# One exponential per wavelength over a ring of two slots, and three wavelengths summed in one column group

## What is computed

```python
cos_pm = jnp.cos(phase_modulators)
def wl_step(acc, wl):
    cpm, iw = wl
    m = cpm[None, :, None, None]
    scores = jnp.einsum('bhqd,bhkd->bhqk', Q * m, K * m) * SCALE
    scores = scores * jnp.cos(KERR * scores * scores)      # KERR = 2.7e-12
    attn = jax.nn.softmax(scores, axis=-1)
    out = jnp.einsum('bhqk,bhkd->bhqd', attn, V)
    return (acc + out * iw, None)
acc, _ = jax.lax.scan(wl_step, acc0, (cos_pm, interference_weights))
...
x = _layernorm(x + attention(x)); x = _layernorm(x + experts(x))
```

## Time and profile before

| | |
|---|---|
| time, median of 3 runs | 7213.8 us (7212.1 to 7214.84) |
| time of the profiled execution | 7212.97 us |
| its span, first to last instruction | 7211.4 us |
| ScalarE busy | 6960.2 us, 97% |
| VectorE busy | 5712.5 us, 79% |
| TensorE busy | 5963.4 us, 83% |
| mean granted TensorE clock | 0.942 of 2.4 GHz |

### The profile page before, as it was taken

How to read it: one execution, slowest core, us unless ns; L and a number is a source line. 1 busy time by engine, 2 the same in 40 slices (tenths; PEclk the granted TensorE clock), 3 DMA queues, 4 the chain that set the end, 5 groups by cost and what they waited for, 6 DMA issues and landing times.

```text
span 7211.4 us, 126028 instructions
## 1 busy us (share of the span) xinstructions
PE 5963.4 (83%) x46020; PEld 2136.2 (30%) x46020; DVE 5712.5 (79%) x7952; ACT 6960.2 (97%) x2227; POOL 116.5 (2%) x243
## 2 busy tenths in 40 slices
PE   6788787877888888888888888888888888888877
PEld 2222222222232333332332332332332332332335
DVE  4777778777788888888888888888888888888873
ACT  3999999999999999999999999999999999999992
POOL 0000000000000000000000000000000000000000
PEclk7999999999999999999999999999999999999998
DMA  2000000000010010010100010000110000000101
GB/s 59 4 4 3 4 4 4 2 4 7 24 29 20 24 29 22 21 29 20 30 29 19 24 29 17 27 29 16 30 31 18 27 28 15 29 26 19 29 18 36
DMA packets 61110, 151.22 MB, mean 21 GB/s; under 512 B 10272, under 2 KB 28576, under 8 KB 60320
## 3 DMA queue, kind: packets, MB, share of 16 engines
q1 hardware_dynamic: 59808, 142.14, 6.9%
q0 software_dynamic: 768, 1.57, 0.1%
HBM read 132.66 MB, written 11.01 MB: 20 GB/s over the span
## 4 chain that ended last, share of the span: by engine, by line
ACT 54%; issue 25%; PE 10%; ACTq 6%; DVE 4%; DMA 0%; SPq 0%; DVEq 0%
ACT ring L558 54%; PE pv L627 5%; ACTq L553 5%; DVE scores L768 1%; ACTq L554 1%; PE sc L1094 1%; PE tr L1102 1%; PE pv L634 1%; PE sc L610 1%; ACT L572 0%; ACTq L546 0%; PE sc L591 0%; DMA scores<-in_L_attn_x 0%; DVE vprobs L793 0%; DVE vprobs L792 0%
## 5 line engine op out<-in xcount | busy, mean ns | idle before, releaser
L558 ACT ACTIVATE ring<-scores 128x4096 f32<-128x4096 f32 (+3 forms) x2048 | 6752.4, 3405 | 40.3 <-DVE scores L768 32.8
L627 PE MATMUL pv<-ring,vh 128*32 128x512 f32 x30720 | 4023.3, 638 | 1131.4 <-ACT ring L558 1120.3
L627 PEld LDWEIGHTS pv<-ring,vh 128*32 128x32 f32 x30720 | 1009.9, 115 | 3810.8 <-issue 2119.1
L800 DVE COPY numer<-pv 128x512 f32<-128x512 f32 x512 | 352.6, 689 | 487.3 <-PE pv L634 482.9
L768 DVE COPY scores<-sc 128x1024 f32<-128x1024 f32 (+1 forms) x512 | 602.2, 1218 | 82.3 <-PE sc L610 79.4
L758 DVE TENSOR_REDUCE rowmax<-sc 128x1 f32<-128x1024 f32 x512 | 601.9, 1218 | 50.5 <-PE sc L591 49.1
L794 DVE SCALAR_TENSOR_TENSOR vprobs<-ring,vprobs 128x1024 f32<-128x1024 f32 x512 | 627.3, 1225 | 17.6
L793 DVE SCALAR_TENSOR_TENSOR vprobs<-vprobs,vbits 128x1024 f32<-128x1024 f32 x512 | 627.3, 1225 | 17.4
L792 DVE SCALAR_TENSOR_TENSOR vprobs<-ring 128x1024 f32<-128x1024 f32 x512 | 623.3, 1217 | 2.9
L634 PE MATMUL pv<-vpower,vlast 128*32 128x512 f32 x2048 | 532.3, 595 | 0.0
L634 PE MATMUL pv<-vprobs,vlast 128*32 128x512 f32 x2048 | 529.6, 592 | 0.0
(11 more groups left out here) (158 smaller groups left out, 2669.8 us busy)
## 6 DMA issues: line engine op xcount, KB each, us to landing
tile_w<-in_L_ffn_w SPq DMA_DIRECT2D x192, 512.0 KB, 3.9
qt<-q_scratch SPq DMA_DIRECT2D x256, 36.0 KB
kt_<-k_scratch SPq DMA_DIRECT2D x256, 36.0 KB
ring<-in_L_ffn_w SPq DMA_DIRECT2D x2, 2048.0 KB, 11.8
scores<-in_L_attn_x SPq DMA_DIRECT2D x4, 512.0 KB, 5.2
q_scratch<-qt SPq DMA_DIRECT2D x4, 512.0 KB, 3.8
k_scratch<-kt_ SPq DMA_DIRECT2D x4, 512.0 KB, 4.2
v_scratch<-vv SPq DMA_DIRECT2D x4, 512.0 KB, 3.7
```

The lines of the kernel that those rows point to most:

```text
L558: nc.scalar.activation(ring[:, i % SLOTS, 0:cols], scores[:, bass.ds(n % 2, 1), half * CK:(half + 1) * CK, :].rearrange("p o k s -> p (o k ...
L627: last = nc.tensor.matmul(sums, vh[:, buf, half * CK + k, :], ring[:, 2 * half + w2, col:col + HALF], start=(half == 0 and k == 0), stop=( ...
```

## The change

ScalarE makes all of a wavelength in one activation of 7680 numbers: key tiles 0 to 6, and of tile 7 the first 512 queries. The ring becomes two slots of a whole wavelength. The first activation of a head waits for all eight key tiles of scores, not for four.

VectorE makes the other 512 queries of tile 7 for every wavelength, still two wavelengths at a time: the first operation, whose factor differs, is split in two of 512; the others work on 2 x 512 numbers. Its schedule moves by one step (bit operations in odd steps, polynomials in even ones), and gets a wait for TensorE's step 2 x pair - 3.

TensorE weighs one wavelength a step. The four column groups are now (query half, half of the key tiles); each step has 15 matmuls from the ring and two for VectorE's part, both in the last group. The values stand in `vh` at columns 18 to 26 of 50, zeros around them; a window of 32 columns shifted by 9 puts three wavelengths one below the other in the same 32 partitions, so `pv` is filled and copied once for three wavelengths ("fill"; six a head: 3, 3, 3, 3, 2, 2). Turning a fill also adds the two halves of the key tiles, in a matmul with `fold` in place of the identity (4 matmuls a fill, 64 columns each). `normalise` runs three times a head, on two fills. The products of the tile work get a bank of their own (`tr[:, 1]`) and lose some waits.

```diff
-NCH = 2 * W
 CK = KT // 2
-SLOTS = 4
+SLOTS = 2
+OWN = HALF
+CHUNK = KT * S - OWN
+VR = D + 1
+STACK = 3
+VW = VC + (STACK - 1) * VR
+VAT = (STACK - 1) * VR
+FILLS = ((0, 1, 2), (3, 4, 5), (6, 7, 8), (9, 10, 11), (12, 13), (14, 15))
+NF = len(FILLS)
+FILL_OF = [f for f, ws in enumerate(FILLS) for _ in ws]
+GROUPED = [(f, f + 1) for f in range(0, NF, 2)]
...
-        ring = sb("ring", [P, SLOTS, CK * S])
-        vh = sb("vh", [P, 2, KT, VC])
+        ring = sb("ring", [P, SLOTS, KT * S])
+        vh = sb("vh", [P, 2, KT, VW])
...
-        vbits = sb("vbits", [P, S], I32)
-        vmant = ring[:, SLOTS - 1, (CK - 1) * S:CK * S]
-        vlast = sb("vlast", [P, 2, 2, VC])
+        vbits = sb("vbits", [P, 2, OWN], I32)
+        vmant = ring[:, :, CHUNK:KT * S]
...
-                    for i in range(8):
-                        pair, half, w2 = i // 4, (i // 2) % 2, i % 2
-                        w, chunk = 4 * quad + 2 * pair + w2, NCH * n + 8 * quad + i
-                        if i in (0, 2):
-                            act.wait_ge(sc_free, USES * n + ROW_USE + 1 + CK * (half + 1))
-                        if half == 0:
-                            act.reg_load(scale[w2], scale_bits[:, bass.ds(w * H + n % H, 1)])
+                    for i in range(4):
+                        w, chunk = 4 * quad + i, W * n + 4 * quad + i
+                        if i == 0:
+                            act.wait_ge(sc_free, USES * (n + 1))
+                        act.reg_load(scale[i % 2], scale_bits[:, bass.ds(w * H + n % H, 1)])
                         act.wait_ge(slot_free, chunk + 1)
                         apart(act)
-
-                        cols = CK * S - (S if half == 1 and w2 == 1 else 0)
-                        nc.scalar.activation(ring[:, i % SLOTS, 0:cols],
-                                             scores[:, bass.ds(n % 2, 1), half * CK:(half + 1) * CK, :].rearrange("p o k s -> p (o k s)")[:, 0:cols],
-                                             ACT.Exp, scale=scale[w2]).then_inc(probs_ready, 1)
+                        nc.scalar.activation(ring[:, i % SLOTS, 0:CHUNK],
+                                             scores[:, bass.ds(n % 2, 1), :, :].rearrange("p o k s -> p (o k s)")[:, 0:CHUNK],
+                                             ACT.Exp, scale=scale[i % 2]).then_inc(probs_ready, 1)
...
+        def weigh_values(pe, n, buf, w):
+
+
+            f = FILL_OF[w]
+            j, pair, w2 = FILLS[f].index(w), w // 2, w % 2
+            first, final = j == 0, w == FILLS[f][-1]
+            window = slice(VAT - j * VR, VAT - j * VR + VC)
+            if w == 0:
                 pe.wait_ge(vh_ready, n + 1)
+            pe.wait_ge(probs_ready, W * n + w + 1 + START)
             for k in range(CK):
                 for g in range(G):
+                    qh, kh = g // 2, g % 2
+                    kt = kh * CK + k
+                    if kt == KT - 1 and qh == 1:
                         continue
+                    last = nc.tensor.matmul(pv[g * VC:(g + 1) * VC, f % 2, :], vh[:, buf, kt, window],
+                                            ring[:, w % SLOTS, kt * S + qh * HALF:kt * S + (qh + 1) * HALF],
+                                            start=(first and k == 0), stop=(final and k == CK - 1))
+            for part, (stream, step) in enumerate(((vpower, POWER_STEP), (vprobs, VSTEPS))):
+                if w2 == 0:
                     pe.wait_ge(vexp_step, VSTEPS * (8 * n + pair) + step)
+                last = nc.tensor.matmul(pv[(G - 1) * VC:G * VC, f % 2, :], vlast[:, buf, part, window],
+                                        stream[:, pair % 2, w2 * OWN:(w2 + 1) * OWN], start=False, stop=(final and part == 1))
+            last.then_inc(slot_free, 1)
+
+        def transpose_numer(pe, n, f):
+            if f % 2 == 0:
+                pe.wait_ge(tr_read, NF // 2 * n + f // 2 + START)
+            pe.wait_ge(pv_read, NF * n + f + 1)
+            for blk in range(4):
+                at = (f % 2) * 4 + blk
+                last = nc.tensor.matmul(tr[:, 0, at * 2 * VC:(at + 1) * 2 * VC], numer[:, blk * P:(blk + 1) * P],
+                                        fold[:, :], start=True, stop=True)
...
-            score = scores[:, bass.ds(m % 2, 1), KT - 1, :].rearrange("p o s -> p (o s)")
-            bits, power = vbits[:, :], vpower[:, pair % 2, :]
+            score = scores[:, bass.ds(m % 2, 1), KT - 1, S - OWN:S].rearrange("p o s -> p (o s)")
+            power = vpower[:, pair % 2, :].rearrange("p (w q) -> p w q", w=2)
             then = stepper(dve, vexp_step, base, [0])
             dve.wait_ge(sc_free, USES * (m + 1))
             if not first:
                 dve.wait_ge(vexp_step, base)
+                dve.wait_ge(slot_free, SLOTS + W * m + 2 * pair - 2)
             apart(dve)
 
-            then(nc.vector.tensor_scalar(bits, score, scales_log2[:, bass.ds((2 * pair + 1) * H + m % H, 1)], LOWEST, ALU.mult, ALU.max))
+            for w2 in range(2):
+                nc.vector.tensor_scalar(vbits[:, w2, :], score, scales_log2[:, bass.ds((2 * pair + w2) * H + m % H, 1)], LOWEST,
+                                        ALU.mult, ALU.max).then_inc(vexp_step, 1)
+            dve.wait_ge(vexp_step, base + 2)
+            then = stepper(dve, vexp_step, base, [2])
+            bits = vbits[:, :, :]
...
+        def copy_numer(dve, n, f):
+
+            dve.wait_ge(slot_free, SLOTS + W * n + FILLS[f][-1] + 1)
+            dve.wait_ge(tr_full, NF * n + f + START)
+            nc.vector.tensor_copy(numer[:, :], pv[:, f % 2, :]).then_inc(pv_read, 1)
+
+        def normalise(dve, n, g):
+
+            js = len(FILLS[GROUPED[g][0]])
+            dve.wait_ge(tr_full, NF * n + 2 * g + 2 + START)
+            blocks = tr[:, 0, :].rearrange("p (m r) -> p m r", r=VC)[:, :, 0:js * VR].rearrange("p m (j c) -> p m j c", c=VR)
+            nc.vector.reciprocal(recip[:, :, 0:js], blocks[:, :, :, D]).then_inc(norm_step, 1)
+            dve.wait_ge(norm_step, NF * n + 2 * g + 1)
+            nc.vector.tensor_tensor(coef[:, :, 0:js], recip[:, :, 0:js], wl_wide[:, g, :, :, 0:js].rearrange("p f t j -> p (f t) j"),
                                     ALU.mult).then_inc(norm_step, 1)
+            dve.wait_ge(norm_step, NF * n + 2 * g + 2)
+            nc.vector.tensor_tensor(parts[:, :, :, STACK * g:STACK * g + js].rearrange("p m d j -> p m j d"), blocks[:, :, :, 0:D],
+                                    coef[:, :, 0:js].rearrange("p m (j o) -> p m j o", o=1).to_broadcast([P, 2 * KT, js, D]),
                                     ALU.mult).then_inc(tr_read, 1)
...
+            for at in range(W):
+                if at in (6, 12):
+                    normalise(dve, n, at // 6 - 1)
+                if at + 1 == W or FILL_OF[at] != FILL_OF[at + 1]:
+                    copy_numer(dve, n, FILL_OF[at])
...
+                pair = (at + 3) // 2
+                step = exponents if at % 2 else polynomials
+                if pair < 8:
+                    step(dve, n, pair)
+                elif more:
+                    step(dve, n + 1, pair - 8)
...
+            exponents(dve, 0, 1)
```

More of the change, by code:

```diff
@@ L64 @@
 LOWEST = -(2.0 ** 30)
-VSTEPS = 7
+VSTEPS = 8
+POWER_STEP = 3
 START = 1
@@ L620, in weigh_values @@
             for k in range(CK):
                 for g in range(G):
-                    qh, w2 = g // 2, g % 2
-                    col = k * S + qh * HALF
-                    sums = pv[g * VC:(g + 1) * VC, pair % 2, :]
-                    if half == 1 and k == CK - 1 and w2 == 1:
+                    qh, kh = g // 2, g % 2
+                    kt = kh * CK + k
+                    if kt == KT - 1 and qh == 1:
                         continue
-                    last = nc.tensor.matmul(sums, vh[:, buf, half * CK + k, :], ring[:, 2 * half + w2, col:col + HALF],
-                                            start=(half == 0 and k == 0), stop=(half == 1 and k == CK - 1))
@@ L629, in weigh_values @@
-            if half == 1:
-                for j, (stream, step) in enumerate(((vpower, 2), (vprobs, VSTEPS))):
-                    pe.wait_ge(vexp_step, VSTEPS * (8 * n + pair) + step)
-                    for qh in range(2):
-                        g = 2 * qh + 1
-                        last = nc.tensor.matmul(pv[g * VC:(g + 1) * VC, pair % 2, :], vlast[:, buf, j, :],
-                                                stream[:, pair % 2, qh * HALF:(qh + 1) * HALF], start=False, stop=(j == 1))
@@ L905, in vector_head @@
-            normalise(dve, n, 3)
+            for at in range(W):
+                if at in (6, 12):
+                    normalise(dve, n, at // 6 - 1)
+                if at + 1 == W or FILL_OF[at] != FILL_OF[at + 1]:
+                    copy_numer(dve, n, FILL_OF[at])
+                if more:
+                    if at < 4:
+                        reduce_max(dve, n + 1, 2 * at)
+                        reduce_max(dve, n + 1, 2 * at + 1)
+                    elif at == 5:
```

(18 more changed lines are left out.)

214 lines of the change are left out of this document (76 added, 138 removed).

## The result

The changed kernel takes 7242.8 us (median of five, 7238.8 to 7253.7) against 7213.7 of the kernel before: a ratio of 1.0043, 95% interval 1.0028 to 1.0058. It is slower by 0.4%, where 0.8% faster was forecast.

The account below looks back on a forecast made before the run. ScalarE's exponentials, coming back to back, were taken to set the time. The terms -95 + 6.8 + 17 + 6 + 5 = -60 us on the profiled 7212.97 gave 7153 us, range 7115 to 7200.

Parts of the forecast that it names:

- One activation in place of two: ScalarE's exponentials: the fixed part of 1024 of 2048 activations goes, less the overlap at the joins, -95 us.
- The first head: Start of the kernel: the first exponential waits for eight tiles of scores instead of four, +6.8 us, once.
- TensorE's steps: Every weighing takes 4.50 us; the chain from part 1's step 12 to step 0 ends 0.7 us late, 24 times: +17 us.
- After the Gelu: Step 4's weighing, slow after TensorE's idleness, makes ScalarE wait 24 times: +10 us, net +6.
- Isolated slow weighings: About 150 weighings at TensorE's lower clock: alone they pass, behind a late step they don't; +5 us, bounds 0 and 45.
- VectorE: VectorE's load stays the same, and its new schedule costs nothing as long as it is less than a step behind.
- VectorE late: Rival: two 512s at full length and `copy_numer` holding TensorE's turning; 1 us a head would be 7215 us; chance 0.02.
- 28 of new waits foreseen: ScalarE's added waits in the sum: 17 behind part 1's slices, 6 after the Gelu, 5 for isolated slow weighings.
- the waits are over 80 us: Sign that the prediction is wrong: ScalarE's waits for slots, forecast at 30 to 40 us in all, exceed 80 us.
- next to none: Sign: ScalarE waits next to none anywhere but behind part 1's last slices and after the Gelu, each under 1.3 us.
- The plain weighings and the beat: Signs: TensorE's weighings of 4.50 us, wrong if over 4.7; ScalarE's activations 6.49 us apart, wrong at another beat.

Follow-up runs that it names:

- e6: Changed kernel with TensorE's two loops written out as Python loops and VectorE's end of the tile moved from step 13 to 15: 7138.0 us (0.9897).
- e5: Changed kernel with TensorE's two loops written out as Python loops, so that it jumps back nowhere: 7185.9 us (0.9965).
- e4: Changed kernel with VectorE's last layer norm of a tile moved from step 13 to step 15, behind its copy: 7207.9 us (0.9991).
- e3: Kernel before with hint_back_edge set to False on TensorE's two loops: 7362.2 us (1.0207).
- e11: Kernel before with 36 no-operations written into the body of TensorE's loop: 7213.8 us (1.0).
- e12: Kernel before with 72 no-operations written into the body of TensorE's loop: 7213.0 us (1.0).
- e13: Kernel before with 8 small matmuls a head added on TensorE, four records each: 7236.1 us (1.0032).

## Why the prediction was wrong

*One activation in place of two: held.* -95 was forecast, -90.8 measured (the exponentials' busy time: 6663.1 for 6752.4 us, -89.3). Activations take 6.60 us for 6.58. The beat, from e6's

```profile
3688.78 104.05 ACT L570 ACTIVATE ring<-scores 128x7680 f32<-128x7680 f32 x16
```

is (104.05 - 6.60) / 15 = 6.50 for 6.49. The overlap at the joins, which I took from the earlier trace rows, is what kept the gain from being 190.

*The first head: held in sign, +4.7 for +6.8.* The wait for scores grew by 7.5 (40.3 against 32.8); the rest of the start took 2.8 less.

*TensorE's steps: held.* Every plain weighing takes 4.50 us. Late by 0.86, 1.00, 1.80 and 2.56 us at steps 13, 14, 15 and 0, for 0.85, 0.94, 1.74 and 2.54. One wait of 0.64 in each of 24 pairs, 15.4 us, for 24 x 0.7 = 17; one of them:

```profile
3676.68 13.11 ACT L570 ACTIVATE ring<-scores 128x7680 f32<-128x7680 f32 x2 [0.64 <-PE pv L648]
```

*After the Gelu: held.* 8.7 us for 10, none above 1.14. The slow weighing there takes 5.8 to 7.4 us, at a granted clock of 0.58 to 0.77 over its length, for its first part ran at the lower clock.

*Isolated slow weighings: nothing where 5 us stood.* None but those behind a late start costs a wait. I had written that ("behind a late step they don't" pass) and put 5 us on all of it. There are 65 slow ones instead of 172, probably by TensorE's shorter idleness; the mean clock is 0.962 for 0.942. But 26 of the 65 are at step 0 of an even head, where before has 3, and these are the dear ones. The record of the granted clock has two levels in every run, 1.00 and 0.50 of full speed, one half of the other as the prediction had it.

*VectorE: this step failed.* Its load was right (5657.0 us busy, 55 under before). The sentence "all this costs nothing as long as VectorE is less than a step behind" was not. The copy of the last sums isn't covered by a step: TensorE's turning and the next head's first weighing queue behind it. TensorE idles meanwhile, comes back at the lower clock (0.64 to 0.83 over the weighing in e5), and the weighing takes 0.9 to 2.5 us more. 1.74 us late is far less than a step of 6.49, and it costs 1.3 to 3.0 us wherever that weighing is slow (21 of 23 boundaries of e5), and nothing where it isn't. The rival *VectorE late* named this very wait (`copy_numer` holding TensorE's turning), but as something spread over the heads, at 0.02. I weighed it by busy time. Its place could have been seen in the timeline of before, where the copy is 1.2 us late whenever step 15's weighing in the second loop is a plain one. It is worth 35 us alone, and 48 where there are no long jumps (e6 against e5).

*The jump back: no step at all.* The parts cover weighings, slices, turnings and copies, not the loop around them. Before shows it as 0.16 us of issue, and nothing there tells that it could be 3.3 us and more. It is worth 57 us, or 70 where the copy isn't late (e6 against e4).

Without both, 7138.0 stands against my 7153; the 15 us are mainly 28 of new waits foreseen against 12 that came (18.2 less 6.0).

Of the signs by which I meant to tell, two spoke: the waits are over 80 us, and 80% of them stand at a place that I had as "next to none". The plain weighings and the beat gave no sign.

## What to carry to other kernels

When an edit shortens the beat of the bounding engine, walk through the loop's edge as a step of its own: the last copy, the last turning, the jump and the first work behind it, and ask what each has to spare in the timeline of before, not how busy its engine is. A jump of TensorE took 0.4 or 3 to 4 us here, and an edit that changes nothing inside the loop can switch it; measure a variant with the loop written out, or moved, before judging a change of under 1%. A delay that looks small beside a step can cost more than its length, if TensorE comes back from the idleness at the lower clock, as it did here (0.64 to 0.83 in e5); and causes that meet at one place have to be tested one by one and together, since here both cost 105 us, where each alone cost 48 and 70.

## What the runs showed of the hardware

- TensorE's jump back took 0.34 to 0.49 us or 3.3 us and more. Without the hint 29 of 29 were long, with it 0, 14 or 17 to 23; 64 or 128 real records ahead of unchanged loops took 17 to 0.
- What a long jump cost went by what followed. In e3 jumps of 101 us made 149 us: 22 of the 29 have a second stop of 2.9 us behind them, and the weighings behind these ran at a granted clock of 0.53 to 0.64.
- Where 3.5 to 7.0 us lay between the end of one weighing and the start of the next, with only the turning and the jump between them (after and e5, from head 18 on), the next took 5.4 to 7.4 us instead of 4.50 in 43 of 46 cases, at a granted clock of 0.60 to 0.83. In a plain step, with 2.0 us between them, it took 4.50, at 1.00.
- A 512-number operation of VectorE takes 479 ns where 1024 took 747: 211 ns of it don't shrink, so two of them cost 211 ns more than one, as I had taken (0.2). The product with strided output at L820 takes 876 ns for 384 numbers.
- The turning with 64 columns takes 1.10 us for 8 records, no less than with 128 (1.04).
- No-operations written for TensorE left neither record nor change in the fetches (382 pieces in before, e11 and e12). Eight small matmuls a head did: 64 records more a turn, and 412 pieces (e13).
